# Attention with graph hops, one core: q and k projected in one product, operands copied within SBUF, calls reordered per head

## The reference

```python
xn = layer_norm(layernorm(x), gamma_in)
q = heads(xn @ Wq) * 64 ** -0.5          # (b, 16, 1024, 64)
k, v = heads(xn @ Wk), heads(xn @ Wv)
attn = softmax(where(causal, q @ k.T, -max))
out = attn @ v
adj = clip(attn + eye, 0, 1); deg = adj.sum(-1)
feats = v
for l in range(2):
    h = feats @ gnn_w[l] + gnn_b[l]
    feats = gelu((adj @ h) / deg + feats)
out = out + feats @ lin_w + lin_b
x = x + layernorm(layer_norm(out @ Wo, gamma_out))
# second stage: two layers of local attention and a gated feed-forward block
```

## Time and profile before

| | |
|---|---|
| median of 3 runs | 1625.44 us |
| the profiled execution, in all | 1620.1 us |
| its span, first to last instruction | 1618.3 us |
| TensorE busy | 1469.1 us (91%) |
| VectorE busy | 1285.7 us (79%) |
| ScalarE busy | 1054.1 us (65%) |
| GpSimd busy | 419.2 us (26%) |
| granted clock of TensorE, mean | 0.972 |

### The profile page before, as it was taken

The page is one execution under the profiler, slowest core; times in us unless marked ns, Lnnn a source line. Parts: engine busy times, 40 slices in busy tenths (PEclk is TensorE's granted clock), DMA queues, the critical chain, the costliest instruction groups (busy, mean ns, idle before and its releaser), DMA issues.

```text
span 1618.3 us, 30002 instructions
## 1 busy us (share of the span) xinstructions
PE 1469.1 (91%) x10578; PEld 1157.4 (72%) x10578; DVE 1285.7 (79%) x3374; ACT 1054.1 (65%) x2403; POOL 419.2 (26%) x544
## 2 busy tenths in 40 slices
PE   5999999999999999999999999998467899999996
PEld 4678877788788887788877888777245566666664
DVE  6588887888888788888888888875577888878875
ACT  3577676666676767767667676764245777787673
POOL 2122223222332222322233222211322342223221
PEclk9899999999999999999999999999778999999999
DMA  4000000000000000000000000000400010000100
GB/s 122 1 1 2 1 1 1 1 1 1 1 1 1 1 1 1 1 1 1 1 1 1 2 1 1 1 1 1 111 14 20 17 26 19 21 21 17 28 18 20
DMA packets 23199, 19.67 MB, mean 12 GB/s; under 512 B 8414, under 2 KB 18314, under 8 KB 23050
## 3 DMA queue, kind: packets, MB, share of 16 engines
q1 hardware_dynamic: 23050, 17.76, 4.3%
HBM read 8.84 MB, written 1.05 MB: 6 GB/s over the span
## 4 chain that ended last, share of the span: by engine, by line
issue 33%; PE 27%; DVE 20%; ACT 10%; POOL 8%; DMA 0%; SPq 0%; POOLq 0%; DVEq 0%; ACTq 0%
ACT t L1213 5%; PE PS L671 3%; DVE t L1554 2%; PE PS L672 2%; PE PS L706 2%; POOL t L1307 2%; DVE t L1585 2%; POOL t L1350 2%; PE PS L618 2%; PE PS L581 2%; POOL t L1340 2%; PE PS L619 1%; DVE t L1756 1%; DVE t L1782 1%; DVE t L1740 1%
## 5 line engine op out<-in xcount | busy, mean ns | idle before, releaser
L1061 ACT ACTIVATE t<-PS 128x512 f32<-128x512 f32 (+3 forms) x384 | 191.3, 498 | 222.3 <-PE PS L621 136.5
L1554 DVE TENSOR_TENSOR t<-t 128x512 fp32r<-128x512 f32 (+3 forms) x384 | 246.6, 642 | 48.8 <-ACT t L1062 47.3
L1532 DVE TENSOR_REDUCE t<-PS 128x1 f32<-128x512 f32 (+3 forms) x384 | 208.0, 549 | 24.2 <-PE PS L581 24.0
L1062 ACT ACTIVATE t<-PS 128x512 fp32r<-128x512 f32 (+3 forms) x384 | 191.7, 499 | 0.0
L1350 POOL TENSOR_TENSOR t<-t 128x256 f32<-128x256 f32 x64 | 39.2, 613 | 551.7 <-DVE t L1574 551.7
L671 PE MATMUL PS<-t 128*128 128x512 f32 (+3 forms) x384 | 141.8, 369 | 21.6 <-ACT t L1095 21.6
L1213 ACT ACTIVATE t<-PS,t 128x128 f32<-128x128 f32 x256 | 113.2, 464 | 67.4 <-DVE t L1786 67.3
L1415 POOL TENSOR_TENSOR t<-t 128x16 f32<-128x16 f32 x32 | 92.8, 2900 | 239.7 <-DVE t L1742 239.7
L636 PE MATMUL PS<-t 128*66 128x512 f32 (+3 forms) x384 | 137.3, 358 | 16.2 <-DVE t L1554 16.2
L581 PE MATMUL PS<-t 128*128 128x512 f32 (+3 forms) x384 | 141.0, 378 | 3.6 <-DVE t L1532 2.7
L618 PE MATMUL PS<-t 128*128 128x512 f32 (+3 forms) x384 | 143.6, 374 | 0.1
(11 more groups left out here) (191 smaller groups left out, 4152.6 us busy)
## 6 DMA issues: line engine op xcount, KB each, us to landing
t<-t SPq DMA_DIRECT2D x60, 128.0 KB, 2.3
t<-in_L_ffn_wqkv SPq DMA_DIRECT2D x2, 768.0 KB, 6.9
t<-in_L_attn_Wv SPq DMA_DIRECT2D x2, 512.0 KB, 7.9
t<-in_c_rot SPq DMA_DIRECT2D x2, 512.0 KB, 4.7
out<-t SPq DMA_DIRECT2D x4, 256.0 KB, 2.3
t<-in_L_ffn_w SPq DMA_DIRECT2D x2, 341.0 KB
t<-in_L_attn_x SPq DMA_DIRECT2D x2, 256.0 KB, 3.2
t<-in_L_attn_Wq SPq DMA_DIRECT2D x1, 512.0 KB, 5.5
```

What stands on the lines that cost most here:

```text
L1061: e.activation(Es[:, k % NS, 0:n], b[:, 0:n], ACT.Exp).then_inc(a_es.up((t, k)), 1)
L1062: e.activation(Eh[:, o:o + n], b[:, 0:n], ACT.Exp).then_inc(a_eh.up((t, k)), 1)
L1532: e.tensor_reduce(n[:, c, ib:ib + 1], bank(k % 2)[:, 0:hi - lo], AX.X, ALU.max, negate=True).then_inc(d_max.up((t, k)), 1)
L1554: e.tensor_tensor(El[:, o:o + n], Es[:, k % NS, 0:n], f32(Eh[:, o:o + n]), ALU.subtract).then_inc(d_el.up((t, k)), 1)
```

## The change

The weights of k and q stand side by side in one matrix (k in the columns 0 to 63, q in 64 to 127), so one product gives k in the lower and q in the upper half of the partitions. ScalarE rounds it with a factor per partition (qsc: 1 and 0.125) into K1; VectorE writes the low parts of both to Q1. SyncE then lays out the operands by eight transfers per head (part and double): K1[64:128] (q high) to Q2[0:64], Q1[0:64] (k low) to K2[0:64], and once these have landed, K1[0:64] (k high) to K1[64:128] and Q2[0:64] (q high) to Q1[0:64]. K1 is then (k high, k high), Q1 (q high, q low).

The maxima are no longer split: nm, [128, 8], is transposed by one fp32 matmul to [8, 128], copied to MR, and a transfer lays it out as the one row Q2[64]. K2 and Q2 have 65 rows.

GpSimd's upper is gone, and its widen writes 64 columns in place of 128. smax waits for both doubled halves (twice), scores also for the row (row_ready). The order of the calls within a turn is new on TensorE, VectorE, ScalarE and GpSimd. Core of the diff:

```diff
+            def part(t):
+                r = t % RB
+                for c in range(2):
+                    sl = slice(c * 512, (c + 1) * 512)
+                    q.wait_ge(*a_hi[t, c])
+                    e.dma_start(f32(Q2[r][0:64, sl]), f32(K1[r][64:128, sl])).then_inc(s_apart[c], 16)
+                    q.wait_ge(*d_low[t, c])
+                    e.dma_start(f32(K2[r][0:64, sl]), f32(Q1[r][0:64, sl])).then_inc(s_apart[c], 16)
+
+            def double(t):
+                r = t % RB
+                for c in range(2):
+                    sl = slice(c * 512, (c + 1) * 512)
+                    q.wait_ge(*apart(t, c))
+                    e.dma_start(f32(K1[r][64:128, sl]), f32(K1[r][0:64, sl])).then_inc(s_twice[c], 16)
+                    e.dma_start(f32(Q1[r][0:64, sl]), f32(Q2[r][0:64, sl])).then_inc(s_twice[c], 16)
+
+            def mrow(t):
+                q.wait_ge(*a_row[t])
+                e.dma_start(f32(Q2[t % RB][64:65, :]).rearrange("a (k p) -> a k p", k=8), f32(MR[:])).then_inc(s_row, 16)
+
+            part(0)
+            double(0)
+            for t in range(NH):
+                if t + 1 < NH:
+                    part(t + 1)
+                mrow(t)
+                if t + 1 < NH:
+                    double(t + 1)
...
-            def proj(t, which, c, b):
+            def proj(t, c, b):
                     q.wait_ge(*a_eh[t - 2, 10 + c])
-                    q.wait_ge(*d_max[t - 1, 10 + c])
-                e.matmul(bank(b), WD[t % RB][:, 0, i, :], xh[:, x0_:x1_], start=True, stop=False)
-                e.matmul(bank(b), WD[t % RB][:, 1, i, :], xh[:, x0_:x1_], start=False, stop=False)
-                e.matmul(bank(b), WD[t % RB][:, 0, i, :], xl[:, x0_:x1_], start=False,
-                         stop=True).then_inc(p_proj.up((t, which, c)), 1)
+                W = WD[t % RB]
+                e.matmul(bank(b), W[:, 0, :], xh[:, x0_:x1_], start=True, stop=False)
+                e.matmul(bank(b), W[:, 1, :], xh[:, x0_:x1_], start=False, stop=False)
+                e.matmul(bank(b), W[:, 0, :], xl[:, x0_:x1_], start=False, stop=True).then_inc(p_proj.up((t, c)), 1)
...
-                q.wait_ge(*d_low[t, "q", 1])
-                q.wait_ge(*a_hi[t, "k", 1])
+                q.wait_ge(*twice(t, 0))
+                q.wait_ge(*twice(t, 1))
...
-            def mrow(t, c):
+            def mrow(t):
                 q.wait_ge(*d_nm[t])
-                q.wait_ge(*d_ident["R"])
-                if c:
-                    q.wait_ge(*a_row[t, 0])
-                elif t:
-                    q.wait_ge(*a_rt[t - 1, 1])
-                else:
-                    q.wait_ge(*d_low[1, "k", 1])
-                for k in range(4):
-                    m = e.matmul(bank(4)[0:66, k * P:(k + 1) * P], NM[:, 4 * c + k, :], identR[:], start=True, stop=True)
-                m.then_inc(p_row.up((t, c)), 1)
+                q.wait_ge(ld["id"], 16)
+                q.wait_ge(*(a_rt[t - 1, 1] if t else d_low[1, 0]))
+                e.matmul(bank(4)[0:8, 0:P], nm[t % 2][:, 0, :], identF[:], start=True, stop=True).then_inc(p_row.up(t), 1)
...
-                q.wait_ge(*a_row[t, 1])
-                q.wait_ge(*w_q2[t, 1])
-                q.wait_ge(*d_low[t, "q", 1])
-                q.wait_ge(*d_low[t, "k", 1])
+                q.wait_ge(*row_ready(t))
+                q.wait_ge(*twice(t, 0))
+                q.wait_ge(*twice(t, 1))
...
                 scores(t, 10)
-                smax(t + 1, 9)
+                av(t, 6)
                 graph1(t, 0)
+                graph2(t - 1, 11)
+                smax(t + 1, 11)
+                scores(t, 11)
+                smax(t + 1, 10)
+                av(t, 9)
+                proj(t + 2, 0, 2)
                 graph2b(t - 1)
-                av(t, 6)
-                scores(t, 11)
-                av(t, 9)
-                smax(t + 1, 11)
-                smax(t + 1, 10)
+                proj(t + 2, 1, 3)
                 av(t, 7)
-                proj(t + 2, "q", 0, 2)
                 av(t, 8)
                 av(t, 10)
                 av(t, 11)
-                proj(t + 2, "q", 1, 3)
-                proj(t + 2, "k", 0, 0)
-                mrow(t + 1, 0)
+                graph2(t, 0)
                 graph1(t, 1)
-                proj(t + 2, "k", 1, 1)
-                graph2(t, 0)
                 graph2(t, 2)
-                mrow(t + 1, 1)
+                mrow(t + 1)
                 graph2(t, 1)
                 graph2(t, 3)
                 graph2(t, 4)
...
-            def mrow(t, c):
-                q.wait_ge(*p_row[t, c])
-                e.copy(Q2[t % RB][64:66, c * 512:(c + 1) * 512], bank(4)[64:66, :]).then_inc(a_row.up((t, c)), 1)
+            def mrow(t):
+                q.wait_ge(*p_row[t])
+                if t:
+                    q.wait_ge(*row_ready(t - 1))
+                e.copy(MR[:], bank(4)[0:8, 0:P]).then_inc(a_row.up(t), 1)
...
-            def lower(t, which, c, b):
-                r = t % RB
-                sl = slice(c * 512, (c + 1) * 512)
-                q.wait_ge(*a_hi[t, which, c])
+            def lower(t, c, b):
+                r, sl = t % RB, slice(c * 512, (c + 1) * 512)
+                q.wait_ge(*a_hi[t, c])
                 q.wait_ge(*p_sc[t - RB, NTL - 1])
-                if which == "k":
-                    m = e.tensor_tensor(K2[r][0:64, sl], bank(b)[0:64, :], f32(K1[r][0:64, sl]), ALU.subtract)
-                else:
-                    m = e.scalar_tensor_tensor(Q1[r][64:128, sl], bank(b)[64:128, :], 0.125, f32(Q1[r][64:128, sl]),
-                                               ALU.mult, ALU.subtract)
-                m.then_inc(d_low.up((t, which, c)), 1)
+                e.scalar_tensor_tensor(Q1[r][:, sl], bank(b), qsc[:, 0:1], f32(K1[r][:, sl]), ALU.mult,
+                                       ALU.subtract).then_inc(d_low.up((t, c)), 1)
...
-                q.wait_ge(*p_row[t - 1, 1])
-                e.tensor_tensor(n[:, 0, 4:8], n[:, 0, 4:8], n[:, 1, 4:8], ALU.min).then_inc(own.up(), 1)
-                q.wait_ge(*own.now())
-                e.tensor_copy(NM[:, :, 64], n[:, 0, :]).then_inc(own.up(), 1)
-                q.wait_ge(*own.now())
-                e.tensor_tensor(NM[:, :, 65], n[:, 0, :], f32(NM[:, :, 64]), ALU.subtract).then_inc(d_nm.up(t), 1)
+                e.tensor_tensor(n[:, 0, 4:8], n[:, 0, 4:8], n[:, 1, 4:8], ALU.min).then_inc(d_nm.up(t), 1)
...
                 scores(t, 10)
-                smax(t + 1, 9)
                 graph1(t, 0)
+                scores(t, 11)
                 graph2b(t - 1)
-                scores(t, 11)
+                feats(t, 0)
+                lower(t + 2, 0, 2)
+                lower(t + 2, 1, 3)
                 smax(t + 1, 11)
+                share(t, 0)
                 smax(t + 1, 10)
-                feats(t, 0)
-                lower(t + 2, "q", 0, 2)
-                lower(t + 2, "q", 1, 3)
-                share(t, 0)
-                lower(t + 2, "k", 0, 0)
                 graph1(t, 1)
-                lower(t + 2, "k", 1, 1)
                 feats(t, 1)
...
```

232 lines of the change are left out of this document (102 added, 130 removed).

## The result

The changed kernel takes 1609.9 us (median of four runs, 1609.5 to 1610.6) where the kernel before takes 1625.4 in the same session: ratio 0.9905, 95% interval 0.9888 to 0.9922. It is 15 us faster; 1577 was expected, and 1609.9 lies outside the range of 1550 to 1608. Its profiled execution took 1610.55 us, span 1608.7.

What follows compares the result with a forecast made beforehand. TensorE was taken to bound the head, matmuls end to end but for two waits: 31.75 us a head, 1.67 less, in 30 heads. 1620.1 - 50 + 2 = 1572, with 5.3 carried over 1577 us; range 1550 to 1608.

Steps and rivals of the forecast that it cites:

- rival E: TensorE isn't what the head waits for; removed work becomes waiting, head stays at 33.3 to 33.5 us; chance 0.04.
- TensorE work removed, 1.8 us a head: Projections 1.40 and row of maxima 0.48 less, new row matmul 0.12 more, fewer length changes 0.05 less: 32.0 to 30.2.
- (a): Wait at hopend and the copy behind it, ahead of graph2(t, 4): unchanged, 0.84 us a head.
- (b): Wait ahead of graph1(t, 1) for the copy L1069, now with less cover: 0.3 us a head.
- (c): Wait at smax(t+1, 11) for VectorE's maximum of smax 9: 0.25 us a head.
- (d): Wait at scores 2 and 3, which follow the first exps closer than before: 0.1 us a head.
- (e): The 0.54 us wait for subtraction L1554 goes; a lock with L1371 may delay feats(t, 0) and row minimum 1.2, hidden.
- (f): Row of maxima, from mrow through copy and transfer: there at 31.3 us, asked for at 31.75, hidden with 0.4 to spare.
- Rival D: The row's transfer, behind the operands' on one queue, takes over; slower kernel, 1642 us at 5 us landing; chance 0.09.
- (g): Doubled operands for smax(t+2, 0): landed at 33.1 us, asked for at 33.9, hidden with 0.7 to spare.
- rival C: Late operands: L1371 strikes feats(t, 0), row or doubled halves land 0.5 to 1 us later; 1594 to 1621; chance 0.15.
- Start, +2: Unhidden first transfers, smax(0) taking some 6 us, scores(0, 0) at about 41 us: +2 us (-1 to +8).

Runs made afterwards that it cites:

- the one-pass run: Changed kernel with the row matmul in the one-pass format instead of full fp32 in two passes: 1595.3 us, ratio 0.9815.
- the dealt-out run: Changed kernel with six long projection matmuls and eight short second-hop matmuls alternating instead of grouped: 1602.3 us, ratio 0.9874.
- kernels of five edits: Changed kernel plus later loads, matmuls at start, one-pass row, hop-tile swap, transposes ahead: 1588.7 us; with fewer added matmuls and transposes split: 1576.3 us.

## Why the prediction was wrong, point by point

- **What bounds the head** (TensorE's line, no other engine): right for the new order. Two matmuls less gave 0.24 us each, so rival E falls. For the order of before, from which it was read, it was half right: there six gave 0.11 each.
- **TensorE work removed, 1.8 us a head**: this term failed. With the waits taken out, the head of before has 32.03 us of steps and the changed one 30.99, 1.04 less. The projections gave 1.42, as counted. The row gave 0.16 for 0.36: its fp32 matmul has two passes, 0.31 us, of which the one-pass run takes back 0.17. The prediction had read two passes from L657 and then counted one. On the other side 0.54 us were lost, spread over steps of other matmuls that have new neighbours: graph2 +0.4, scores +0.2, all others together -0.1. The 0.05 that I had counted as a gain from fewer changes of length had the wrong sign. Which neighbour does it, isn't settled; the dealt-out run shows that long behind short isn't dear as such.
- **Waits**: (a) 0.84, right. (b) 0.3, right, 0.33. (c) 0.25 at smax 11, right in the usual head, 0.29; but 0.7 more in the eight heads and 0.2 more in seven others in which VectorE has other tiles to do. The prediction had laid out one head and multiplied by 30. (d) none, for 0.1. (e) the 0.54 is gone, right. In all 1.45 us in the usual head for the 1.49 laid out. The lock that was told for feats(t, 0) does occur, with the GpSimd operation before the one named: L1586 takes 0.85 us, where its shortest takes 0.41, beside GpSimd's L1372, which began 0.73 us before it. Those 0.4 us are hidden, since the row minimum is written by 612.99 and the row's matmul starts at 613.79:

```profile
609.03 1.29 POOL L1372 TENSOR_TENSOR t<-t 128x512 f32<-128x512 f32 x1
...
609.76 0.84 DVE L1586 TENSOR_TENSOR t<-t 128x256 fp32r<-128x256 f32 x1
```

- **(f) the row's transfer, hidden**: right; TensorE never waits for it in the loop. Rival D falls. Its one landing that can be seen is at the start: issued at 43.55, it releases scores(0, 0) at 45.45, 1.9 us for the 2.3 taken. That is nearer the 2.0 that the prediction takes from the Trainium skill, whose section fits it to transfers issued by GpSimd; these are SyncE's.
- **(g) the doubled operands, hidden with 0.7 to spare**: right in two heads of three. SyncE needs 0.60 us for an issue and not the 0.46 of the earlier trace rows, so the spare is 0.4; and a landing of 4 us, which the earlier trace rows had shown as its slowest, 4.3 of 60, was taken for a rare one. It comes with TensorE's instruction fetch, five times in three heads, and one in five hits. 8.2 us. That is the late landing of rival C, by another cause, and not its lock: the lock alone cost nothing.
- **Start, +2**: +13.9 at the first product. The first four transfers, behind the loads, landed by 29.0, near the 28 told, but smax(0) took 9 us for the 6 told, until 42, and scores(0, 0) started at 45.45 for the 41 told. The lower clock is a part of this only: at the full clock, in the kernels of five edits, smax(0) still took 7.2 us, with a matmul added behind each maximum. Yet the first av stood only 0.8 us later than before (50.5 for 49.8). The other 13 us came behind it: some 10 from the lower clock up to 74 us, 3 from the order. Longer idling was named as what "could lengthen that stretch", and the range for it, +8, was too small.
- **5.3 us carried over from profile to median**: wrong in kind. The profiled execution of before, 1620.1 us at a mean clock of 0.972, was a fast one of its kind; eleven runs of before in the last session spread from 1619.5 to 1627.7 with mean clocks of 0.973 to 0.967. The changed kernel's profiled execution stands at its own median.
- **The sum**: the loop gained 24.5 us for 50. Thirty heads x 0.69 are 21 us too much, the slow heads 8, the longer waits for VectorE in fifteen heads 4; against this stand 3 us more from the two heads of 35.5 us, which are now 32.9, and some 4 more in the last three stretches, 25.5 in all. With the start's 12 and the end's 1 that is the 38 us between the 1572 told for the profiled execution and 1610.6. The 5.3 carried over hid 5 of them: 1577 is 33 us short of the median, not 38, by luck.

## What to carry to other kernels

Lay out the new order in steps, but price a removed matmul together with its neighbours: take one or two out of the kernel as it is and time that, before a price times a count. A transfer that is hidden by less than 2 us isn't hidden if it recurs in every turn: something in the loop will fall on it, here the fetch of another engine's instructions, and then 84 waits more in that engine's stream or 0.9 us of independent work ahead of its reader are worth 8 us. Look at every kind of head, not one: a wait that is 0.3 us in the usual head was 1.0 in eight others. Where TensorE idles at the start, count on the time at the lower clock behind it, 24 to 51 us in the traces with 6 to 10 us of idling ahead of smax(0), and not on the idle time alone.
